# Scatter-adds of a mixture of experts, ordered only where the expert changes

## The reference

```python
rh = relu(features @ router_w1 + router_b1)          # features: x normalised, 6250 x 256
top_w, top_i = top_k(softmax(rh @ router_w2 + router_b2), 2)     # 2 of 6 experts
routing_weights = softmax(top_w)
expert_out = three dense layers of 256 x 256, one set for each expert
x = x + sum over the two chosen experts of expert_out * routing_weight
```

## Time and profile before

| | |
|---|---|
| median of 3 runs | 2712.95 us (2711.92 to 2713.81) |
| profiled execution | 2712.23 us |
| its span, first to last instruction | 2710.5 us |
| mean granted TensorE clock | 0.901 of full speed |
| busy share of the span: PE, PEld, DVE, ACT, POOL | 83%, 70%, 68%, 52%, 50% |
| expert stage, first load to the end of the span | 2332.2 to 2710.5 us |

### The profile page before, as it was taken

How to read it: one execution, slowest core, us unless ns; L and a number is a source line. 1 busy time by engine, 2 the same in 40 slices (tenths; PEclk the granted TensorE clock), 3 DMA queues, 4 the chain that set the end, 5 groups by cost and what they waited for, 6 DMA issues and landing times. The chain is left out here.

```text
span 2710.5 us, 48967 instructions
## 1 busy us (share of the span) xinstructions
PE 2244.7 (83%) x11258; PEld 1887.1 (70%) x11258; DVE 1843.9 (68%) x6399; ACT 1403.4 (52%) x3945; POOL 1362.1 (50%) x1281
## 2 busy tenths in 40 slices
PE   2888676999958989999898899899899663598895
PEld 1444355999957778887787788788787563487774
DVE  7877789777756777777777777777777652144442
ACT  3566474222206666666666676666676651133331
POOL 1000000111147777777777777777777178344444
PEclk9999877999959999998999999999999765699998
DMA  4100000100023333333333333333333354244443
GB/s 146 36 26 27 16 12 19 49 18 19 18 52 106 106 108 107 106 106 109 105 105 109 104 105 105 109 105 105 110 106 102 114 144 131 73 77 82 80 83 48
DMA packets 130088, 223.02 MB, mean 82 GB/s; under 512 B 37607, under 2 KB 80660, under 8 KB 129820
## 3 DMA queue, kind: packets, MB, share of 16 engines
q0 software_dynamic: 78864, 160.18, 24.4%
q1 hardware_dynamic: 49418, 58.93, 7.3%
q10 hardware_dynamic: 1538, 1.31, 0.2%
HBM read 171.72 MB, written 49.77 MB: 82 GB/s over the span
## 5 line engine op out<-in xcount | busy, mean ns | idle before, releaser
L1197 POOL DMA_INDIRECT area<-wh_table,area x1004 | 1012.7, 1009 | 319.5 <-issue 299.4
L1424 PE MATMUL bank<-area 128*126 128x258 f32 x2008 | 513.7, 401 | 2.1 <-DVE acc_mem L1308 1.2
L1424 PEld LDWEIGHTS bank<-area 128*126 128x126 f32 x2008 | 379.8, 199 | 55.8 <-ACT area L1369 2.6
L509 POOL DMA_INDIRECT sorted_slots<-area x28 | 46.6, 1663 | 720.6 <-issue 485.8
L1369 ACT ACTIVATE area<-area 128x126 f32<-128x126 f32 x1004 | 318.8, 388 | 135.2 <-issue 121.2
L1415 PEld LDWEIGHTS bank<-area 125*128 125x128 f32 x2008 | 272.5, 203 | 161.8 <-issue 126.7
L1226 DVE TENSOR_SCALAR area<-iota_row,area 128x126 f32<-128x126 f32 x1004 | 360.1, 364 | 21.4 <-DVE area L1219 4.1
L1415 PE MATMUL bank<-area 125*128 125x2 f32 x2008 | 261.4, 252 | 113.2 <-DVE area L1298 112.0
L1360 ACT ACTIVATE area<-iota_row,area 128x126 f32<-128x126 f32 x1004 | 316.2, 389 | 0.1
L1346 ACT ACTIVATE area<-bank 125x512 f32<-125x512 f32 x251 | 149.5, 596 | 262.1 <-DVE area L1236 258.9
L1902 POOL DMA_INDIRECT out_dram<-area x108 | 170.2, 1576 | 205.9 <-DMA out_dram<-area 122.8
(11 more groups left out here) (325 smaller groups left out, 3980.5 us busy)
## 6 DMA issues: line engine op xcount, KB each, us to landing
area<-wh_table,area POOLq DMA_INDIRECT x1004
area<-moe_rows SPq DMA_DIRECT2D x54, 264.0 KB, 2.7
wh_table<-area SPq DMA_DIRECT2D x50, 126.0 KB
xn<-in_x_dram SPq DMA_DIRECT2D x25, 250.0 KB
x_rows<-area SPq DMA_DIRECT2D x25, 250.0 KB
area<-x_rows SPq DMA_DIRECT2D x25, 250.0 KB
area<-in_L_ffn_expert_w_dram SPq DMA_DIRECT2D x3, 1536.0 KB, 11.7
out_dram<-xn SPq DMA_DIRECT2D x2, 1500.0 KB
```

The source lines that it names most:

```text
L1197: g.indirect_dma_start(out=gath[:, s % RG, t, :], out_offset=None, in_=table, in_offset=bass.IndirectOffsetOnAxis(ap=idx_tab[:, s * GT + t ...
L1424: last = T.matmul(bank[US][0:RW, 0:WROW], sm[:, b, t, :], gath[:, j % RG, t, :], start=(t == 0), stop=(t == GT - 1))
```

## The change

Three semaphores, one for each `yo` buffer, count the additions in place of one. They are those of the routing stage (`sent`), which stand at `sent_rows` when the expert stage begins. landed(j) is the value that tile j's semaphore has when both its additions have landed.

POOL no longer waits for earlier additions. Where two neighbouring tiles belong to different experts, VectorE waits instead: weighed(j) waits for tile j - 1 if the expert of j differs from that of j - 1, and for tile j - 2 if it differs from that of j - 2. As the program is unrolled and the experts are only known at run time, the waits are always there, against a register that is loaded from one of two new tables, `clear1` and `clear2`. Where the expert is the same the value is 32 lower, which is the landing of the tile three earlier on that semaphore. Seven small instructions make the tables in the routing stage: three iotas on POOL, and two comparisons and two multiply-adds on VectorE, with one more wait of VectorE for itself. SP waits for the same additions as before, on the new semaphores. The end of the program waits for the last three tiles.

```diff
@@ -1474,6 +1474,7 @@
         ej_i, base_i = take(MT).bitcast(I32), take(MT).bitcast(I32)
+        clear1, clear2 = take(MT).bitcast(I32), take(MT).bitcast(I32)
@@ -1503,6 +1504,7 @@
         ej_f, base_f = take(MT), take(MT)
+        gone, change = take(MT), take(2, MT)
@@ -1539,6 +1541,12 @@
+        sent_rows = [16 * 2 * sum(SIZES[g] for g in range(NS) if g % PB3 == b) for b in range(PB3)]
+
+        def landed(j):
+
+            return sent_rows[j % PB3] + 32 * (j // PB3 + 1)
@@ -1585,6 +1593,9 @@
+                for b in range(PB3):
+                    g_.iota(gone.rearrange("p (a b) -> p a b", b=PB3)[:, :, b], pattern=[[32, MT // PB3]], base=sent_rows[b],
+                            channel_multiplier=0, allow_small_or_imprecise_dtypes=True)
@@ -1724,6 +1735,10 @@
                 V.tensor_scalar(ej_i, ej_f, float(NX - 1), None, ALU.min)
+                V.tensor_tensor(change[:, 0, 1:MT], ej_f[:, 1:MT], ej_f[:, 0:MT - 1], ALU.not_equal)
+                step(V.tensor_tensor(change[:, 1, 2:MT], ej_f[:, 2:MT], ej_f[:, 0:MT - 2], ALU.not_equal))
+                V.scalar_tensor_tensor(clear1[:, 1:MT], change[:, 0, 1:MT], 32.0, gone[:, 0:MT - 1], ALU.mult, ALU.add)
+                V.scalar_tensor_tensor(clear2[:, 2:MT], change[:, 1, 2:MT], 32.0, gone[:, 0:MT - 2], ALU.mult, ALU.add)
                 step(V.tensor_scalar(base_i, base_f, float(NX * REG), None, ALU.min))
@@ -1876,7 +1891,6 @@
-        added = sem("added")
@@ -1888,7 +1902,7 @@
                     if j >= RB6:
-                        sp.wait_ge(added, 32 * (j - RB6 + 1))
+                        sp.wait_ge(sent[(j - RB6) % PB3], landed(j - RB6))
@@ -1896,18 +1910,18 @@
                     g.wait_ge(d_y, 2 * j + 2)
-                    if j > 0:
-                        g.wait_ge(added, 32 * j)
                     for s in range(2):
                         g.indirect_dma_start(
...
-                                             compute_op=ALU.add).then_inc(added, 16)
-                g.wait_ge(added, 32 * MT)
+                                             compute_op=ALU.add).then_inc(sent[j % PB3], 16)
+                for j in range(MT - PB3, MT):
+                    g.wait_ge(sent[j % PB3], landed(j))
...
                 regs = [dve.alloc_register(f"expert{i}") for i in range(4)]
+                clears = [dve.alloc_register(f"clear{i}") for i in range(4)]
@@ -1943,9 +1957,17 @@
                 def weighed(j):
                     e = expert(j)
+                    held = []
+                    for back, clear in ((1, clear1), (2, clear2)):
+                        if j >= back:
+                            k, reg = (j - back) % PB3, clears[2 * (j % 2) + back - 1]
+                            dve.reg_load(reg, clear[0:1, j:j + 1])
+                            held.append((sent[k], dve.snap(reg, min_val=sent_rows[k], max_val=landed(j - back))))
+                    for other, value in held:
+                        dve.wait_ge(other, value)
                     dve.wait_ge(t_d, j + 1)
                     if j >= 3:
-                        dve.wait_ge(added, 32 * (j - 2))
+                        dve.wait_ge(sent[j % PB3], landed(j - PB3))
```

More of the change, by code:

```diff
@@ L55 @@
 RB6 = 6
-assert sum(SIZES) == NT and max(SIZES) == ST and len(SIZES) == NS
+assert MT % PB3 == 0 and sum(SIZES) == NT and max(SIZES) == ST and len(SIZES) == NS
 assert COLS * L >= E and HI <= L and HI * LO < 2 ** 14
```

## The result

| | before | after |
|---|---|---|
| median | 2712.69 us, 6 runs (2710.16 to 2716.29) | 2665.84 us, 6 runs (2660.69 to 2670.15) |
| profiled execution | 2712.23 us | 2670.15 us |
| its span | 2710.5 us | 2668.4 us |
| first load of the expert stage to the end | 2332.2 to 2710.5: 378.3 us | 2335.4 to 2668.4: 333.0 us |
| first to last start of the scatter line | 344.5 us | 298.8 us |

The ratio of after to before is 0.9823 (95% interval 0.9812 to 0.9834): 1.8% faster. The forecast was 2666.0. The profiled execution after the change happens to be the slowest of its six. It entered the expert stage 3.2 us later than the one before; the stage itself is 45.3 us shorter.

A forecast was written before the change was run, and what follows sets the result against it. POOL's loop with the DMA, 6.42 us a tile, held PE; without its wait PE's 5.62 sets the pace. The last scatter moves from 2699.1 to 2652.4 (-46.7 us), giving a 2666 us median, range 2661 to 2690.

The forecast's parts named there:

- the loop's 6.42: Expert stage before: POOL's issue, the DMA landing and POOL's wake take 6.42 us a tile, against PE's 5.62.
- The sum: Expert stage: tile 53's scatter starts at 2652.4 in place of 2699.1, -46.7 us; median 2666 us.
- the end's terms: Last tiles: POOL's issues, tile 52's landing at 2651.3, DVE's wake and result put the last scatter at 2652.4.
- The waits at the changes: DVE's results where the expert changes: five inner ones 1.13 us late, 2.5 to spare, so free; the last one counts.
- The register loads and waits: weighed on DVE: two loads and waits take 0.65 us a tile, 1.15 at most, inside 2.63 us idle time.
- Landings under more traffic: Scatter landings: stay near 3.8 us at DMA share 0.57; by the skill possibly 1.8 longer, giving 2670 us.
- rival 1: Scatter landings stretch once POOL no longer waits: 2668 us at 4.8 us each, 2694 at 9.0; chance 0.10.
- The 9.0: Worst landing in the routing stage, 9.0 us; if reached in the expert stage, the total is 2694 us.
- rival 2: PE's clock in the expert stage falls to 0.91 under full load, giving 2696 us; chance 0.06.
- rival 3: weighed waits for the previous tile's landing at every tile: 6.75 us a tile, 15 us late, 2728 us; chance 0.04.
- rival 4: DVE's register waits are dear, some 5.3 to 6 us a tile, so time stays at 2713 us; chance 0.03.
- six waits of DVE for the DMA at most: Expert stage sign: DVE waits for DMA in at most six places, about 1 us each, the last some 3.

The follow-up runs named there:

- semonly: Kernel before with the three new semaphores, POOL still waiting for each earlier tile's landing; 2713.85 us, ratio 0.9995 to before.
- always1: bounded with the first comparison always true, so every tile waits for the landing of the tile before; 3074.00 us, ratio 1.0129 to the kernel before.
- halfdown: Changed kernel without the second half of the contraction in `down` (four of eight matmuls); 2998.19 us, ratio 0.9789 to before; first to last scatter 276.7 us.
- bounded: Changed kernel plus one register operation (lower bound 0) before each of the two register waits; base of the variants; 2667.01 us, ratio 0.9828 to before.
- static: Changed kernel with weighed's register loads and waits replaced by constant waits at the six tiles where experts change; 2667.10 us, ratio 0.9822 to before.
- clamped: bounded with tables made from the limited expert number, so empty tile 53 counts as expert 5; 2664.43 us, ratio 0.9821 to before.
- staticpool: static with its constant waits moved to POOL, ahead of its issues; 3014.06 us, ratio 0.9848 to the kernel before on the same chip.
- more4: bounded with four more used register loads a tile, each with a move and comparison; 3037.87 us, ratio 0.9920 to before; first to last scatter 320.0 us.
- more10: bounded with ten more used register loads a tile, each with a move and comparison; 3169.49 us, ratio 1.0349 to before; first to last scatter 451.4 us.

## Why the prediction was right

**The bound.** PE's 5.62 us a tile took the place of the loop's 6.42, as forecast: the windows are full, the chain is on PE, semonly and always1 show that POOL's wait alone made the loop, and halfdown that the time moves with PE's work, by half of what is taken off. The second limit is closer than I wrote: at 5.2 us ACT's work between `mid` and `up` is next; DVE would be at some 4.1, an estimate (3.0 of its own and up to 1.1 for the loads).

**The sum.** Forecast -46.7 us in the stage. Measured, from tile 0's `down` to tile 53's scatter: 2356.58 to 2656.50 is 299.9 where it was 345.7 (2353.41 to 2699.11), so -45.8. The offset of 3.17 added to the forecast's times, down(51) was due at 2642.77 and started at 2642.72. The missing 0.9 are in the end's terms: POOL starts 0.27 to 0.28 after a result, which I left out and which counts twice, at tile 51 (tile 52's issue began at 2649.62 where 2649.27 was due) and at tile 53; tile 52's first issue took 1.68, not 1.56; and its landing took 3.59, not 3.36, with 0.14 until DVE started, not 0.20. What follows the last scatter took 11.9 us, not 11.4. That makes -45.3 to the span's end. The median moved by -46.85, which fits the sum better than its parts justify: the stages ahead of this one move a run by more than that difference. In the six profiles before, changed, bounded, static, clamped and semonly the first load came at 2332.2, 2335.4, 2331.7, 2332.2, 2326.8 and 2337.5, with no link to what was changed.

**The waits at the changes.** I had at most 1.13 us late against 2.5 us to spare. They were 0.6 to 1.4 late, and free all the same. What I left out is POOL's 0.27 after a result; at tile 32, 0.35 came with tile 31's own delay. DVE's start after a landing was shorter than my 0.20, 0.14 at tile 53. static and staticpool confirm it.

**The register loads and waits.** Taken at 0.65 us a tile, which was too little, and bounded by 1.15; the runs put them at 0.8, and at 1.1 at most. A register load's row shows its own 0.303 us, not what its issue and the moves behind it add. It cost nothing, since it stayed under 2.63.

**Landings under more traffic.** 3.9 in the median, 5.3 at most. At a DMA share of 0.54 to 0.59 the median grew by 0.1. The longest landing says nothing for rival 1: semonly, with one tile at a time as before, had one of 5.4. The 9.0 never came. By the Trainium skill (DMA: Bandwidth & Descriptors, Latency and other measured facts) a landing could have grown by 1.8 us under high load, an estimate; no run here shows that in the median.

**The clock.** It stayed at 1.00 through the 237 us of unbroken matmuls from 2403 to 2640, so rival 2 had no place. This agrees with the Trainium skill (TensorE: Matmul & The Clock Gate, What's actually happening): activity releases the throttle. The 0.91 of the earlier trace rows came from something else, which no run here separates.

**What was wrong in the text.** Two steps, neither of which moved the number. In rival 3 the loop of 6.75 was 7.22 in always1: 43 us above before (421.7 less 378.3 in the stage), not 15. In the changed kernel itself, with 6.96, it would be some 30, an estimate. In rival 4 I added the 2.5 us that a single late result may take to DVE's idle time at every tile. A delay that the next tile makes good is room once; a cost that comes back with every tile has only the 2.63. more4 and more10 show it. The table's other side, too: I forecast six waits of DVE for the DMA at most, and the profile names 26; the starts show six.

## What to carry to other kernels

A wait for the previous transfer's completion puts the whole latency into each turn; if only a few known places need the order, keep it there, and put the wait on an engine with idle time. Check two kinds of room separately: what a single late step may borrow from the steps behind it, and what every turn may cost. When a wait is removed, add up the next engine's time per turn from a stretch in which it already ran without a gap; here such a stretch stood in the profile of before, and it gave the new time to 1 us in 46.

## What the runs showed of the hardware that was not expected

- A register load on DVE is 0.30 us in its row but costs 0.41 to 0.44 us of the engine's time together with the moves and comparison behind it (2.87 us idle with six, 5.49 with twelve).
- A landing wakes a waiting POOL after 0.71 us and a waiting DVE after 0.14 us where that wait is the sequencer's last (changed kernel) and after 0.40 where three more steps follow it (bounded).
- The same kernel before took 2713, 3038 and 3063 us on three chips, with mean granted clocks of 0.90, 0.87 and 0.86. The expert stage, unrolled and fed by plain and indirect DMAs, took the same time on the first two (298.7 to 299.2 us for programs that do the same in it); on the third no such program was profiled, but staticpool's results start 5.62 us apart there too. The difference lies ahead of the stage, and its cause is open.
- In more10, where PE is busy in 38.92 of 50 us, the granted clock fell to 0.91 and below; in always1, busy in 39.62 of 50, it was 1.00 in every window up to 3030 us. One window of each, and one `down` of each from the timelines:

```profile
2780.00:2830.00 50.00, 38.92 (x166) 32.26 (x165) 15.76 (x51) 12.93 (x30) 17.50 (x12) 0.91 0.40 65
```

```profile
2795.68 3.68 PE L2075 MATMUL bank<-area 128*128 128x256 f32 x8 [3.02 <-DVE area L1951]
```

```profile
2780.00:2830.00 50.00, 39.62 (x190) 33.48 (x189) 19.82 (x63) 15.11 (x35) 20.51 (x14) 1.00 0.42 70
```

```profile
2791.67 1.99 PE L2071 MATMUL bank<-area 128*128 128x256 f32 x8 [2.14 <-DVE area L1951]
```

  The busy shares are nearly equal only because the lower clock stretches more10's matmuls: it did 166 in its window where always1 did 190, and the `down` behind an idle piece of 3.02 us took 3.68 us. In always1 the one behind 2.14 us took 1.99. So more10's PE has both less work and longer idle pieces; which of them decides was not tried.
